# Row statistics in three groups of 8, 8 and 16 tiles in place of two of 8 and 24

## The chip, the core and the metric

The kernel runs on one core of a Trainium2 chip. The metric is the device time of one execution in microseconds (us); lower is better. The engines are called PE (TensorE, matmuls), DVE (VectorE), ACT (ScalarE), POOL (GpSimd) and SP (SyncE, which here issues all DMAs). Each engine has a queue of its own and works through it in order; engines wait for each other by semaphores.

## The reference

x is 8 batches x 512 rows x 128 columns in float32. All of it passes one block:

```python
xn = _layernorm(x)                        # (x - mean) / sqrt(var + 1e-5)
s = attention(xn)                         # relu(xn @ Wq + bq), K and V alike; 16 heads of 8,
                                          # causal, masked where a row of xn sums to 0; + xn; normalised
g = _silu(ffn(xn))                        # second layernorm of xn, @ attn_w.T + attn_b + xn, then by
                                          # 256 rows one of 8 experts: gelu(. @ w1 + b1) @ w2 + b2,
                                          # then gelu(. @ next_w.T + next_b)
return x + s * g
```

The mask asks whether a row of xn sums to exactly 0, so the kernel computes xn with a square root and a quotient refined from split high and low parts, and that costs many instructions.

## The kernel before

**Tiles and parts.** The 4096 rows are 32 tiles of 128 rows; a batch is 4 tiles (`TB`). The program has two parts with a barrier between them. The first prepares everything by batch: xn, the q and k rows (each split into three bf16 parts and stored in DRAM), v, and the gate g for all rows. The second runs the attention of the 8 batches and writes the output. The change is in the first part alone.

**DVE in the first part.** All helpers record their instructions through `link`, which makes DVE wait for the end of each instruction before it starts the next one (L313 to L317; in `quotients` only the last of four instructions that belong together is linked). They are:

- `variances(group)`, L321 to L335: row sums, mean, centred rows and variance of all tiles of a group. `row_sum` (L78 to L87) is 5 of its 13 instructions. Four of the 13 run over all columns of the group (L81, L328, L329, L330), the others over a few numbers for each tile.
- `roots(group)`, L337 to L357: square root and reciprocal, in the Newton helper (L67 to L75, 14 instructions with three steps) and 15 more. All work on one column for each tile.
- `second_roots(group)`, L377 to L384: what the second layernorm needs, 4 instructions and the Newton helper's 14.
- `quotients(i)`, L359 to L375, gives xn of batch i and releases PE's transposes. `sums(i)`, L386 to L395, gives its row sums and releases ACT's second layernorm (`sums_ready`). `rests` (L397 to L402) and `lows` (L404 to L409) are DVE's share of splitting q and k: `rests` waits for ACT's `full` and `parts[0]` (L498, L499), `lows` waits for ACT's middle part (L517) and releases SP's stores (`low_ready`). `gate(i)` (L411 to L417) finishes the gate.

`GROUPS` (L31) says which tiles are handled together: 8 tiles (batches 0 and 1), then 24 (batches 2 to 7). The order on DVE is written out by hand (L419 to L447): group 0 with `variances`, `roots`; batch 0 with `quotients`, `second_roots(GROUPS[0])`, `sums`; batch 1; the rests of batch 0; `variances(GROUPS[1])`; the low parts of batch 0; `roots(GROUPS[1])`; then a loop over the batches i = 2 to 7. A turn is `quotients(i)`, the rests of batch i-1, `sums(i)`, `gate(i-2)`, and the low parts of batch i-1; the turn of batch 2 has `second_roots(GROUPS[1])` ahead of its sums.

**The other engines.** SP loads x by group (L232 to L240), after the first group the rows of biases, after the second the weights, and behind the loop `w1` and `w2` (L241, L242). Then, by batch, it waits for `low_ready` and stores the parts of q (3 DMAs) and k (5 DMAs), and from the third batch on it also loads query and key rows for the attention part. ACT copies q and k of a batch out of PSUM (L498, L499) only when the stores of the batch before have landed (`parts_out`), then v (L503), then the experts' gelus (L511) with the middle parts between them (L517, after `rest_ready`), then the second layernorm of the next batch (L459). PE's second half of the experts (L598, h = 1) waits for v to be out of its bank (`vb_free`). Then come the transposes of the next batch (L548, L542), the products L553 and L555, q (L579) and k (L580).

Of the kernel before, what the change touches and what calls it, by code (L numbers as in the profile page):

```python
# [26 lines left out]
NT = B * T // P  # L27
TB = T // P
STEPS = B // MB
MT = NT // MB  # L30
GROUPS = ((0, 2 * TB), (2 * TB, NT - 2 * TB))  # L31
EC = T // 2
HC = HID // P
G = 4
# [32 lines left out]
def rsqrt_newton(link, dve, y, t, a, steps):  # L67

    link(dve.tensor_scalar(t.bitcast(I32), a.bitcast(I32), 1, None, ALU.logical_shift_right))  # L69
    link(dve.tensor_scalar(y.bitcast(I32), t.bitcast(I32), -1, RSQRT_SEED, ALU.mult, ALU.add))  # L70
    for _ in range(steps):
        link(dve.tensor_tensor(t, y, y, ALU.mult))
        link(dve.tensor_tensor(t, t, a, ALU.mult))
        link(dve.tensor_scalar(t, t, -0.5, 1.5, ALU.mult, ALU.add))
        link(dve.tensor_tensor(y, y, t, ALU.mult))  # L75


def row_sum(link, dve, total, s16, s8, s4, s2, src):  # L78

    add = dve.tensor_tensor  # L80
    link(dve.tensor_reduce(s16, src.rearrange("p n (k l) -> p n l k", l=16), AX.X, ALU.add))  # L81
    v = s16.rearrange("p n (a b l) -> p n a b l", a=2, b=2)
    link(add(s8, v[:, :, :, 0, :], v[:, :, :, 1, :], ALU.add))
    link(add(s4, s8[:, :, 0, :], s8[:, :, 1, :], ALU.add))
    v = s4.rearrange("p n (a b) -> p n a b", b=2)
    link(add(s2, v[:, :, :, 0], v[:, :, :, 1], ALU.add))
    link(add(total, s2[:, :, 0], s2[:, :, 1], ALU.add))  # L87
# [7 lines left out]
def build_program(nc, ctx, x, wq, wk, wv, wattn, wnext, w1, w2, cols, rows, out):  # L95
# [3 lines left out]
    def sem(name):  # L99
        return ctx.enter_context(nc.semaphore(name))  # L100
# [64 lines left out]
    with ExitStack() as one:  # L165
# [37 lines left out]

        x_in = [sem(f"x_in{k}") for k in range(len(GROUPS))]
        rows_in, bias_ready = sem("rows_in"), sem("bias_ready")
# [23 lines left out]
        with nc.Block() as block:  # L229
            @block.sync  # L230
            def _(sp):
                for k, (t0, n) in enumerate(GROUPS):  # L232
                    sp.dma_start(x_all[:, t0:t0 + n, :], x_tiles[:, t0:t0 + n, :]).then_inc(x_in[k], 16)
# [76 lines left out]
            def _(dve):  # L310
                chain = [0]

                def link(ins):  # L313

                    chain[0] += 1
                    ins.then_inc(dve_self, 1)
                    dve.wait_ge(dve_self, chain[0])  # L317
# [3 lines left out]
                def variances(group):  # L321

                    t0, n = group
                    at = slice(t0, t0 + n)
                    xg = x_all[:, at, :]
                    row_sum(link, dve, mean[:, at], s16[:, at, :], s8[:, at, :, :], s4[:, at, :], s2[:, at, :], xg)
                    link(dve.tensor_scalar(mean[:, at], mean[:, at], 1.0 / C, None, ALU.mult))
                    link(tt(cen[:, at, :], xg, mean[:, at].unsqueeze(2).broadcast_to([P, n, C]), ALU.subtract))  # L328
                    link(tt(work[:, at, :], cen[:, at, :], cen[:, at, :], ALU.mult))  # L329
                    link(dve.tensor_reduce(win[:, at, :], work[:, at, :].rearrange("p n (w k) -> p n w k", k=32),  # L330
                                           AX.X, ALU.add))
                    link(tt(var[:, at], win[:, at, 0], win[:, at, 1], ALU.add))
                    link(tt(var[:, at], var[:, at], win[:, at, 2], ALU.add))
                    link(tt(var[:, at], var[:, at], win[:, at, 3], ALU.add))
                    link(dve.tensor_scalar(a[:, at], var[:, at], 1.0 / C, 1e-5, ALU.mult, ALU.add))  # L335

                def roots(group):  # L337

                    at = slice(group[0], group[0] + group[1])
                    a_, y_, t_, s_, sh_, sl_, r_, nr_, rem_ = (v[:, at] for v in (a, y, t, s, sh, sl, r, nr, rem))  # L340

                    rsqrt_newton(link, dve, y_, t_, a_, 3)
                    link(tt(s_, a_, y_, ALU.mult))
                    link(dve.tensor_scalar(sh_.bitcast(I32), s_.bitcast(I32), TOP12, None, ALU.bitwise_and))
                    link(tt(sl_, s_, sh_, ALU.subtract))
                    link(tt(t_, sh_, sh_, ALU.mult))
                    link(tt(rem_, a_, t_, ALU.subtract))
                    link(tt(t_, sh_, sl_, ALU.mult))
                    link(dve.scalar_tensor_tensor(out=rem_, in0=t_, scalar=-2.0, in1=rem_, op0=ALU.mult, op1=ALU.add))
                    link(tt(t_, sl_, sl_, ALU.mult))  # L350
                    link(tt(rem_, rem_, t_, ALU.subtract))
                    link(tt(t_, rem_, y_, ALU.mult))
                    link(dve.scalar_tensor_tensor(out=s_, in0=t_, scalar=0.5, in1=s_, op0=ALU.mult, op1=ALU.add))
                    link(dve.tensor_scalar(sh_.bitcast(I32), s_.bitcast(I32), TOP12, None, ALU.bitwise_and))
                    link(tt(sl_, s_, sh_, ALU.subtract))
                    link(dve.reciprocal(r_, s_))
                    link(dve.tensor_scalar(nr_, r_, -1.0, None, ALU.mult))  # L357

                def quotients(i):  # L359

                    tiles = slice(TB * i, TB * i + TB)
                    cu, wu = cen[:, tiles, :], work[:, tiles, :]
                    link(tt(quo[:, :, :], cu, r[:, tiles].unsqueeze(2).broadcast_to([P, TB, C]), ALU.mult))
                    link(dve.tensor_scalar(qhi[:, :, :].bitcast(I32), quo[:, :, :].bitcast(I32), TOP12, None, ALU.bitwise_and))
                    link(tt(qlo[:, :, :], quo[:, :, :], qhi[:, :, :], ALU.subtract))
                    for in0, by, in1, op, dst in (
                            (qhi, sh, cu, ALU.subtract, wu), (qlo, sh, wu, ALU.add, wu),
                            (qhi, sl, wu, ALU.add, wu), (qlo, sl, wu, ALU.add, wu),
                            (wu, nr, quo, ALU.add, xn_all[:, tiles, :])):
                        for k in range(TB):  # L370
                            at = TB * i + k
                            ins = dve.scalar_tensor_tensor(out=dst[:, k, :], in0=in0[:, k, :], scalar=by[:, at:at + 1],
                                                           in1=in1[:, k, :], op0=ALU.mult, op1=op)
                        link(ins)
                    dve.sem_inc(xn_ready, 1)  # L375

                def second_roots(group):  # L377

                    at = slice(group[0], group[0] + group[1])
                    link(dve.tensor_scalar(v2[:, at], var[:, at], 1.0 / C, None, ALU.mult))  # L380
                    link(tt(v2[:, at], v2[:, at], r[:, at], ALU.mult))
                    link(tt(v2[:, at], v2[:, at], r[:, at], ALU.mult))
                    link(dve.tensor_scalar(v2[:, at], v2[:, at], 1e-5, None, ALU.add))
                    rsqrt_newton(link, dve, y2[:, at], t[:, at], v2[:, at], 3)  # L384
# [12 lines left out]
                def rests(tok):  # L397

                    for o in range(2):
                        dve.wait_ge(split_ready, tok.next(split_ready))  # L400
                        link(tt(rest[:, o, :], full[:, o, :], parts[:, o, 0, :], ALU.subtract))
                        dve.sem_inc(rest_ready, 1)  # L402
# [17 lines left out]
                dve.wait_ge(x_in[0], 16)  # L420
                variances(GROUPS[0])
                roots(GROUPS[0])
                quotients(0)
                second_roots(GROUPS[0])
                sums(0)
# [3 lines left out]
                rests(tok)  # L429
                variances(GROUPS[1])  # L430
                lows(tok)
                roots(GROUPS[1])
                for i in range(2, B):
                    quotients(i)
                    rests(tok)
                    if i == 2:
                        second_roots(GROUPS[1])
                    sums(i)
                    if i == B - 1:
                        link(dve.tensor_scalar(live_all[:, :], zero_all[:, :], -1.0, 1.0, ALU.mult, ALU.add))  # L440
                        dve.tensor_scalar(mask_b[:, :], zero_all[:, :], -BIG, None, ALU.mult).then_inc(mask_ready, 1)
                    gate(tok, i - 2)
                    lows(tok)
# [640 lines left out]
```

## Time and profile before

| | before |
|---|---|
| median of 3 runs | 526.83 us (526.40 to 527.27) |
| the profiled execution | 526.47 us, its span 524.7 us |
| PE busy | 437.2 us (83%), 3697 instructions |
| DVE busy | 399.6 us (76%), 976 instructions |
| ACT busy | 302.1 us (58%), 644 instructions |
| POOL busy | 126.5 us (24%), 346 instructions |
| first part (to the barrier) | 0 to 187 us of the span |
| mean granted TensorE clock | 0.942 |

Times in rows are microseconds from the start of the span, unless ns is written. A row of a timeline gives the start, the duration, the engine, the line of the kernel, the operation, the output and input with their shapes, and how many instructions were merged into the row; in brackets stands the idle time before it and what ended that. Gaps between linked instructions of under about 0.15 us are not shown as idle time. "PEclk" is the granted share of TensorE's full clock: 1.00 is 2.4 GHz, 0.50 is 1.2 GHz.

### The profile page before, as it was taken

To read this page: it belongs to the slowest core of one execution; us is meant where nothing else is said; L and a number is where in the kernel's file an instruction comes from. 1 tells how busy PE (TensorE), PEld (TensorE's weight loads), DVE (VectorE), ACT (ScalarE), POOL (GpSimd) and SP (SyncE) were. 2 spreads that over 40 slices of the span, in tenths; PEclk is the share of its full clock that TensorE was granted. 3 is DMA by queue.
4 is the path that set the end of the run, shared out by engine and by line. 5 is a ranking of instruction groups with operands and counts; after the bars stand their busy time and mean duration, and the time that the engine had idled before them with its cause. 6 is when DMAs were issued, how large, how long until landed. Compare 5 with 4: busy or idle time off the path is not lost.

```text
span 524.7 us, 10282 instructions
## 1 busy us (share of the span) xinstructions
PE 437.2 (83%) x3697; PEld 269.2 (51%) x3697; DVE 399.6 (76%) x976; ACT 302.1 (58%) x644; POOL 126.5 (24%) x346
## 2 busy tenths in 40 slices
PE   0049545999999559999999999999999999999980
PEld 0026334767667425555555556556556555555540
DVE  6989998899984267667977877877877877787606
ACT  0029134888787504556666567567567566666670
POOL 8000000000000021011155154164163163162281
PEclk9999957999999955899999999999999999999996
DMA  8900021244443200122312312213323213222000
GB/s 231 296 0 0 11 71 31 60 122 125 126 126 82 81 6 24 51 69 49 93 48 69 92 49 79 82 48 90 74 47 101 61 48 111 52 48 67 3 22 20
DMA packets 27433, 37.60 MB, mean 72 GB/s; under 512 B 5622, under 2 KB 19830, under 8 KB 27382
## 3 DMA queue, kind: packets, MB, share of 16 engines
q1 hardware_dynamic: 27382, 36.94, 25.9%
q8 instruction: 29, 0.48, 0.4%
q14 instruction: 22, 0.18, 0.1%
HBM read 25.91 MB, written 10.49 MB: 69 GB/s over the span
## 4 chain that ended last, share of the span: by engine, by line
PE 53%; DVE 9%; issue 1%; ACT 1%; DVEq 0%; ACTq 0%
PE banks L963 15%; PE banks L994 14%; PE banks L982 12%; PE banks L965 5%; PE banks L984 5%; DVE mx L816 5%; PE banks L1004 1%; DVE stats L863 1%; DVE aggr L867 1%; ACT pt L934 0%; DVE bits L69 0%; DVE seed L70 0%; PE banks L972 0%; DVE half L894 0%; DVE res L850 0%
## 5 line engine op out<-in xcount | busy, mean ns | idle before, releaser
L816 DVE TENSOR_REDUCE mx<-banks 128x1 f32<-128x384 f32 (+3 forms) x384 | 211.1, 597 | 63.6 <-PE banks L965 58.4
L934 ACT ACTIVATE pt<-banks 128x512 f32<-128x512 f32 (+2 forms) x384 | 184.8, 528 | 110.8 <-PE banks L984 99.9
L965 PE MATMUL banks<-causal,ident_b 128*128 128x128 bf16 x512 | 106.8, 228 | 0.0
L984 PE MATMUL banks<-causalT,ident_b 128*128 128x128 bf16 x512 | 103.8, 222 | 0.0
L963 PE MATMUL banks<-k_own,q_own 73*128 73x512 bf16 (+3 forms) x256 | 75.3, 331 | 11.2 <-DVEq L896 8.6
L994 PE MATMUL banks<-pt,vg 128*18 128x512 f32 (+3 forms) x1024 | 82.4, 440 | 0.5 <-ACT pt L934 0.5
L963 PE MATMUL banks<-w_room 73*128 73x512 bf16 (+3 forms) x256 | 69.0, 302 | 3.4 <-DVE mx L816 3.4
L982 PE MATMUL banks<-q_own,k_own 76*128 76x512 bf16 (+3 forms) x256 | 71.1, 310 | 0.0
L982 PE MATMUL banks<-w_room 76*128 76x512 bf16 (+3 forms) x256 | 67.7, 300 | 1.2 <-ACT pt L934 1.2
L726 POOL TENSOR_SCALAR mneg<-mx 128x16 f32<-128x16 f32 x32 | 8.1, 253 | 192.7 <-DVEq L824 192.7
L965 PEld LDWEIGHTS banks<-causal,ident_b 128*128 128x128 bf16 x512 | 52.1, 102 | 0.0
L984 PEld LDWEIGHTS banks<-causalT,ident_b 128*128 128x128 bf16 x512 | 50.9, 99 | 0.2
L963 PEld LDWEIGHTS banks<-k_own,q_own 73*128 73x128 bf16 x256 | 26.2, 104 | 44.3 <-issue 18.7
L598 PE MATMUL banks<-xaT,w_room 128*128 128x256 f32 x128 | 32.3, 400 | 16.9 <-ACT v_all L503 16.9
L994 PEld LDWEIGHTS banks<-pt,vg 128*18 128x18 f32 x1024 | 23.8, 97 | 39.3 <-issue 29.1
L789 POOL MEMSET vg<- 128x1152 f32 x1 | 1.1, 1057 | 173.5 <-POOLq L229 173.5
L963 PEld LDWEIGHTS banks<-w_room 73*128 73x128 bf16 x256 | 24.6, 97 | 33.0 <-DVE mx L816 13.6
L598 PEld LDWEIGHTS banks<-xaT,w_room 128*128 128x128 f32 x128 | 24.3, 199 | 22.3 <-ACT v_all L503 19.3
L610 PE MATMUL banks<-hid,w_room 128*128 128x256 f32 x128 | 32.2, 406 | 3.3 <-ACT hid L511 3.3
L982 PEld LDWEIGHTS banks<-w_room 76*128 76x128 bf16 x256 | 25.0, 98 | 15.6 <-ACT pt L934 4.7
L982 PEld LDWEIGHTS banks<-q_own,k_own 76*128 76x128 bf16 x256 | 25.8, 101 | 12.9 <-ACT pt L934 2.2
L610 PEld LDWEIGHTS banks<-hid,w_room 128*128 128x128 f32 x128 | 25.7, 205 | 8.7 <-ACT hid L511 4.5
(155 smaller groups left out, 581.1 us busy)
## 6 DMA issues: line engine op xcount, KB each, us to landing
k_scratch<-parts SPq DMA_DIRECT2D x40, 128.0 KB, 2.4
q_own<-q_scratch SPq DMA_DIRECT2D x48, 96.0 KB
k_own<-k_scratch SPq DMA_DIRECT2D x48, 96.0 KB
w_room<-q_scratch SPq DMA_DIRECT2D x48, 96.0 KB
w_room<-k_scratch SPq DMA_DIRECT2D x48, 96.0 KB
q_scratch<-parts SPq DMA_DIRECT2D x24, 128.0 KB, 2.4
w_room<-in_w_dram SPq DMA_DIRECT2D x1, 2048.0 KB, 9.2
out_dram<-mixed SPq DMA_DIRECT2D x7, 256.0 KB, 2.5
```

The lines of the kernel that those rows point to most:

```text
L598: ins = mm(banks[:, bank + j // 2, EC * (j % 2):EC * (j % 2) + EC], w1_sb[:, 2 * n + h, P * j:P * j + P], xaT[:, EC * h:EC * h + EC], star ...
L610: ins = mm(banks[:, XB, EC * h:EC * h + EC], w2_sb[:, 2 * n + h, j, :], hid[:, h, j, :], start=(j == 0), stop=(j == HC - 1))
L726: link(pool.tensor_scalar(mneg[:, 0], mx[:, u % 2].rearrange("p h n -> p (h n)"), -1.0, None, ALU.mult))
L816: ins = dve.tensor_reduce(mx[:, u % 2, heads[0]:heads[-1] + 1, q], banks[:, S0 + c % RING, 0:w * len(heads)].rearrange("p (h k) -> p h k", ...
L863: ins = dve.bn_stats(stats[:, k, :], res[:, k, :])
L867: ins = dve.bn_aggr(aggr[:, k, :], stats[:, k, :])
L934: act.activation(weights(k, heads[0], len(heads)), banks[:, ST0 + j % RING, 0:(T - P * k) * len(heads)], ACT.Exp, scale=SCALE).then_inc(ex ...
L963: mm(o, qx[by][0:MROW + 1, g, h, P * q:P * q + P], kx[by][0:MROW + 1, g, h, 0:w], start=True, stop=False)
L965: ins = mm(o[:, w - P:w], ident_b[:, :], causal[:, :], start=False, stop=True)
L982: mm(o, kx[par][0:STACK, g, h, P * k:P * k + P], qx[par][0:STACK, g, h, P * k:T], start=True, stop=False)
L984: ins = mm(o[:, 0:P], ident_b[:, :], causalT[:, :], start=False, stop=True)
L994: ins = mm(banks[32 * h:32 * h + VP, OT, P * k:T], vg[:, g, k, h, :], pt[:, PT0[k] + h * n:PT0[k] + h * n + n], start=(k == 0 and g % 2 == 0),
```

## The change

`GROUPS` gets three entries, so SP loads x with three DMAs (the weights follow the second of them, as before), and there is a third semaphore for the third load. On DVE the second group is now 8 tiles (batches 2 and 3). The remaining 16 tiles (batches 4 to 7) get their load wait, `variances` and `roots` at the top of batch 4's turn, ahead of its quotients, and their `second_roots` in that turn, ahead of its sums. Nothing else is changed, in neither part.

```diff
-GROUPS = ((0, 2 * TB), (2 * TB, NT - 2 * TB))
+GROUPS = ((0, 2 * TB), (2 * TB, 2 * TB), (4 * TB, NT - 4 * TB))
...
                 lows(tok)
                 roots(GROUPS[1])
                 for i in range(2, B):
+                    if i == 4:
+                        dve.wait_ge(x_in[2], 16)
+                        variances(GROUPS[2])
+                        roots(GROUPS[2])
                     quotients(i)
                     rests(tok)
-                    if i == 2:
-                        second_roots(GROUPS[1])
+                    if i % 2 == 0 and i <= 4:
+                        second_roots(GROUPS[i // 2])
                     sums(i)
```

## Rows read from the trace of the kernel before

**Rows 1.** DVE's waits, 4.6 to 163.4: waited for, us in total, times, longest

```profile
DVE s L81 <- DMA x_all<-in_x_dram: 4.6, 1, 4.6
```

**Rows 2.** DVE's waits, 4.6 to 187: the longest of the others

```profile
DVE rest L401 <- ACT parts L499: 7.8, 2, 5.6
```

**Rows 3.** Busy us (instructions) of each engine in one batch's period; clock, DMA share, GB/s

```profile
104.20:118.90 14.70, 14.14 (x69) 10.27 (x68) 13.20 (x36) 12.43 (x27) 0.00 (x0) 1.00 0.43 113
```

**Rows 4.** DVE's timeline: the blocks of 24 tiles, rests and low parts, two batch starts

```profile
45.04 5.37 DVE L81 TENSOR_REDUCE s<-x_all 128x384 f32<-128x3072 f32 x1
...
62.89 1.53 DVE L408 TENSOR_TENSOR parts<-rest,parts 128x512 bf16<-128x512 f32 x2
64.56 0.18 DVE L69 TENSOR_SCALAR small<-small 128x24 int32<-128x24 int32 x1
...
70.95 0.69 DVE L363 TENSOR_TENSOR quo<-xn_all,small 128x512 f32<-128x512 f32 x1
...
78.85 1.53 DVE L401 TENSOR_TENSOR rest<-full,parts 128x512 f32<-128x512 f32 x2
80.53 0.18 DVE L380 TENSOR_SCALAR small<-small 128x24 f32<-128x24 f32 x1
...
84.42 1.00 DVE L81 TENSOR_REDUCE s<-xn_all 128x64 f32<-128x512 f32 x1
...
97.42 1.53 DVE L401 TENSOR_TENSOR rest<-full,parts 128x512 f32<-128x512 f32 x2
...
104.23 0.69 DVE L363 TENSOR_TENSOR quo<-xn_all,small 128x512 f32<-128x512 f32 x1
...
118.94 0.69 DVE L363 TENSOR_TENSOR quo<-xn_all,small 128x512 f32<-128x512 f32 x1
```

**Rows 5.** DVE's timeline: the blocks of the first group, 8 tiles

```profile
4.59 1.86 DVE L81 TENSOR_REDUCE s<-x_all 128x128 f32<-128x1024 f32 x1 [4.59 <-DMA x_all<-in_x_dram]
...
11.44 0.48 DVE L332 TENSOR_TENSOR small<-win 128x8 f32<-128x8 f32 x1
...
12.65 0.25 DVE L69 TENSOR_SCALAR small<-small 128x8 int32<-128x8 int32 x1
...
18.71 0.69 DVE L363 TENSOR_TENSOR quo<-xn_all,small 128x512 f32<-128x512 f32 x1
...
26.61 0.17 DVE L380 TENSOR_SCALAR small<-small 128x8 f32<-128x8 f32 x1
...
30.27 1.00 DVE L81 TENSOR_REDUCE s<-xn_all 128x64 f32<-128x512 f32 x1
```

**Rows 6.** ACT's timeline: split copies of batches 1 and 2

```profile
67.41 0.69 ACT L498 ACTIVATE full<-banks,cols_sb 128x512 f32<-128x512 f32 x1 [11.11 <-DMA q_scratch<-parts]
...
71.28 0.68 ACT L499 ACTIVATE parts<-banks,cols_sb 128x512 bf16<-128x512 f32 x1
...
96.81 0.70 ACT L499 ACTIVATE parts<-banks,cols_sb 128x512 bf16<-128x512 f32 x1
```

**Rows 7.** Busy us in short stretches; the third number from the end is PE's clock

```profile
66.00:69.00 3.00, 0.00 (x0) 0.00 (x0) 2.51 (x15) 1.27 (x2) 0.00 (x0) 0.50 0.73 203
...
90.00:92.00 2.00, 2.00 (x11) 1.85 (x11) 1.90 (x6) 0.97 (x2) 0.00 (x0) 0.56 0.72 197
```

**Rows 8.** PE's timeline: L553 in batches 0 and 2, the hole, attention's first product

```profile
36.28 2.08 PE L553 MATMUL banks<-xlT,wattn_sb 128*128 128x512 f32 x2 [0.87 <-ACT xlT L470]
...
72.50 3.78 PE L598 MATMUL banks<-xaT,w_room 128*128 128x256 f32 x8 [12.88 <-ACT v_all L503]
...
92.07 1.02 PE L553 MATMUL banks<-xlT,wattn_sb 128*128 128x512 f32 x2
...
188.93 0.58 PE L963 MATMUL banks<-k_own,q_own 73*128 73x512 bf16 x1 [8.65 <-DVEq L896]
```

**Rows 9.** DVE's unlinked L372: four merged, then the durations of one (ns, min/median/max)

```profile
72.86 1.14 DVE L372 SCALAR_TENSOR_TENSOR gate_all<-qhi,small,xn_all 128x128 f32<-128x128 f32 x4
...
L372 DVE SCALAR_TENSOR_TENSOR gate_all<-qhi,small,xn_all x32: 346/347/352, 20.6 to 151.1; 128x128 f32<-128x128 f32 x32
```

## The prediction

> **What bounds the kernel now.** The span is 524.7 us, and the edit touches only the part of it ahead of 187 us (preparation and gate); the attention loop behind it is started by a barrier and keeps its work. So I ask which engine sets the length of the first part. I read the list of waits of VectorE (DVE) first [rows 1]: from its first instruction at 4.59 us to 163.4 us it has not one wait but the load of x that it starts with. The reader is to see that this list is empty otherwise: a queue of linked instructions that never waits for another engine is the bound itself. The same list to 187 us [rows 2] adds waits, all of them behind the last batch's rows, the longest 7.8 us for ScalarE's (ACT's) split copies. Then I read the busy times by batch [rows 3], because they could speak against this: in 104.2 to 118.9 us TensorE (PE) is busy 14.14 of 14.70 us, DVE only 13.20. The 1.5 us missing on DVE are the gaps of about 0.03 to 0.15 us between an instruction and the next one that is linked to it; they are part of its pace. The batch period is DVE's own, L363 to L363, 118.94 - 104.23 = 14.71 us [rows 4]. By the code PE waits for ACT in each batch (`vb_free`), ACT for the stores of the batch before (`parts_out`), and SP with those stores for DVE's low parts (`low_ready`). The circle closes at DVE. The end of the first part hangs on DVE as well: the last batch's splits wait for the stores that DVE's second-last low parts release. What is added to DVE's queue before 163.4 us therefore moves the end of the first part one for one, unless DVE is left waiting somewhere, which adds more.
>
> **The change, part by part.**
>
> *Loads.* The third load of x costs SP one more issue, with the weights now behind the second load in place of the third. The first load and its wait are as before. DVE asks for the third group some 50 us later than it asked for all 24 tiles in the kernel before, where the wait showed nothing [rows 1]. I cost it at nothing: the cover is DVE's own work of the first two batches, and if it were gone the price would be one issue, under 1 us.
>
> *One group of 24 becomes 8 and 16.* This repeats `variances` (13 linked DVE instructions: 5 of the row sum, 8 more), `roots` (14 of the Newton helper with three steps, 15 more: 29) and `second_roots` (4 and 14: 18): 60 instructions more. The elements are the same, so what is added is the part of each instruction that doesn't grow with its width. Rows give it by block. `second_roots` takes 84.42 - 80.53 = 3.89 us for 24 tiles [rows 4] and 30.27 - 26.61 = 3.66 us for 8 [rows 5]. On a straight line its part without width is 3.66 - (3.89 - 3.66)/2 = 3.55 us, or 0.197 us for each of 18 instructions. `roots` takes 70.95 - 64.56 = 6.39 and 18.71 - 12.65 = 6.06 us, so 5.90 without width (0.203 each). `variances` takes 62.89 - 45.04 = 17.85 and 12.65 - 4.59 = 8.06 us, so 3.17 without width (0.244 each). The last two are from the kernel's first microseconds, where single instructions were stretched: L332 on 8 columns took 0.48 us [rows 5], more than twice the 0.197. I take the undisturbed rate for all: 60 x 0.197 = 11.8 us. The high end is the sum of the three blocks as they stand, 3.17 + 5.90 + 3.55 = 12.6. The low end gives the four wide instructions of `variances` what L81 shows without width: (5.37 - 1.86)/2 = 1.755 for 1024 columns, 0.11 of 1.86 left, with a gap of 0.03 some 0.14; that is 56 x 0.197 + 4 x 0.14 = 11.6 us.
>
> *What moves.* The 8-tile blocks take about 7.6 and 5.9 us in place of 17.85 and 6.39. The first low parts, which release batch 0's stores, then start near 52.7 in place of 62.89 us, and batch 2's rows begin near 60.2 in place of 70.95. ACT's wait for those stores, now 11.11 us ahead of L498 at 67.41 [rows 6], shrinks, and with it the PE hole behind it. None of that is worth anything: DVE did not wait in that stretch, so what is late next is DVE itself, as before. In exchange the 16-tile blocks (by the line between 8 and 24: 12.7, 6.2 and 3.8 us, 22.7 together) stand in DVE's queue behind batch 2's low parts. Queued behind the first two of them (18.9 us) are batch 4's quotients, batch 3's rests, then its gate and low parts, and behind these SP's stores of batch 3 and its loads of query and key rows. ACT waits for the rests of batch 3, PE for ACT. All of these are off DVE's queue, and DVE gets back to them with its inputs long there.
>
> *Where DVE could be left waiting.* Batch 1's rests (L401) come at 78.85 us and the last split they need ends at 71.28 + 0.68 = 71.96 [rows 6], 9.1 us behind the start of the low parts at 62.89 [rows 4]. After the change the splits end near 52.7 + 9.1 = 61.8, the rests stand at 52.7 + 1.7 + 5.9 + 7.9 = 68.2: margin 6.4, no wait. The margin one batch later is thin. The second of batch 2's two rests starts half of 1.53 and a gap behind 97.42, near 98.26 [rows 4], and the split they need ends at 96.81 + 0.70 = 97.51: 0.75 us [rows 6]. This chain runs from DVE's sums over ACT and PE back to DVE, the DVE work beside it is the same after the change, and batch 4 (behind the new hole) goes through it in the same order. If it keeps its length, the cost is 0. If PE is slower in it, DVE waits.
>
> *The clock in that chain.* PE's granted clock is 0.50 in 66 to 69 us, inside the 12.88 us in which PE had nothing to do ahead of L598 at 72.50, and 0.56 in 90 to 92 us [rows 7, 8]; the products from 92.07 on run at the full rate, 1.02 us for L553 [rows 8]. So in the kernel before this chain runs in part at 1.2 GHz and ends at 2.4. The worst case is what batch 0 had: there the same L553 took 2.08 us [rows 8], 1.06 more. Three such products stand in the chain (L553, L555, L579). Work ahead of them brings the clock back, so I let two of them be slow: 2.1 us, less the margin of 0.75, is 1.4 us for a batch. The change leaves PE with nothing for about 18 us ahead of batch 4, and less than now ahead of batch 2. The Trainium skill ("TensorE: Matmul & The Clock Gate", Part 1, What's actually happening) says that the slow clock is the default and that activity releases it, which speaks against a change that leaves such a hole; by it alone the sum would take this case.
>
> *Sum.* The profiled execution took 526.47 us: 524.7 of span and 1.77 around it. 526.47 + 11.8 + 0 = 538.3. The median of the runs shown is 0.36 higher, 526.83, which gives 538.6 us. I forecast 538.6.
>
> **The rivals.**
>
> *A. The low clock leaves DVE waiting.* As above, at batch 4, at batch 2 or at both: 0 to 1.4 us each, on top of 11.8. For it: the hole, and a margin of 0.75 us only. Against it: the kernel before has a hole of 12.88 us in front of L598 at 72.50 [rows 8] and still kept the margin. Time: 538.6 to 541.4, about 539.6.
>
> *B. PE sets the pace, the other side.* If from 89 us on PE and not DVE were the bound, batch 2's rows 10.9 us earlier would be a gain of 10.9, and the 22.7 us of the 16-tile blocks would be covered by one batch of work in hand, 14.7 us, and cost 8.0: 526.8 - 2.9 = 523.9 us, faster. It decides from the point where the other engines hold more than 22.7 - 10.9 = 11.8 us of work when DVE turns to the third group. For it speaks PE busy 14.14 of 14.70 us [rows 3]. Against it: a DVE queue without a wait [rows 1] can't be ahead of anything; its own instructions fill the time, and 60 more of them can't be put anywhere before the end.
>
> *C. The added instructions overlap.* Four unlinked L372 instructions of 0.347 us each take 1.14 us together [rows 9], so they start (1.14 - 0.347)/3 = 0.26 us apart and hide 0.08 each; if the 60 hid as much and had no gap, they would cost 60 x (0.197 - 0.03 - 0.08) = 5.2 us: 532.0 us. Against it: each of the 60 waits for the end of the one before it by its link, and 18 of them in a row take 3.66 us [rows 5], 0.203 each, with nothing hidden. The Trainium skill ("Vector Engine (DVE) Microarchitecture Reference", section 5.2) states about 75 ns per instruction after queue overlap, by which the sum would be 60 x 0.075 = 4.5 us, some 531.3 us; the trace differs, with 0.197 for linked ones.
>
> **How the numbers follow.** Forecast (11.6 to 12.6 us, no wait on DVE): 0.67. A: 0.28. B: 0.015. C: 0.02. The rest, 0.015, is left for a mishap that I can't name. Forecast with the spread of the runs (526.40 to 527.27): 538.0 to 539.9. To hold 8 in 10, the range must take in more than half of A: up to 540.8, and at the low end a little for wide instructions cheaper than the rows: 537.6. A measurement of this kernel can tell about 0.2% (1.1 us) from no change; B is below that, so faster 0.02; hardly any case lies within it, 0.01; slower 0.97, since the forecast, A and C are all above 527.9.
>
> **What the profile after would show.** The DVE list of waits empty between its first load and a last low part near 175.2 us: right; a row DVE L401 <- ACT L499 at batch 2 or 4 with 0.1 to 1.5 us: case A, with a granted clock near 0.5 beside it. `variances` of 16 tiles near 12.7 us, `roots` 6.2, `second_roots` 3.8, small instructions still 0.20 us apart; 0.1 would be C. Batch 2's quotients near 60 us, those of batch 4 ending near 120, a hole of about 18 us on PE before them. The barrier and the first attention product 11.8 us later than 188.93 [rows 8], and the attention part as long as before. If the first part is not longer by the added DVE time, the reading that DVE is its bound is wrong, and with it the prediction.

## The result and the profile after

The changed kernel takes 537.42 us (median of five runs, 537.30 to 538.34) against 526.83 us (five runs, 526.25 to 527.63). The ratio on record is 1.0213, 95% interval 1.0201 to 1.0225; the plain quotient of the two medians, 1.0201, lies at its lower end. It is slower by about 11 us. The profiled execution took 537.33 us with a span of 535.6 us, 10.9 us over the span before.

The page of the profile after, the lines that answer to the table of before (busy time, share of the span, instructions):

```profile
span 535.6 us, 10343 instructions
...
PE 439.4 (82%) x3697; PEld 271.3 (51%) x3697; DVE 409.1 (76%) x1036; ACT 301.9 (56%) x644; POOL 125.9 (24%) x346
```

The instruction counts say it at once: DVE has 1036 instructions where it had 976, which are the 60 repeated ones; PE, ACT and POOL have theirs unchanged.

DVE's waits, 4.6 to 174 us (answers to [rows 1]), and behind it the longest of the list to 199 us (answers to [rows 2]):

```profile
DVE s L81 <- DMA x_all<-in_x_dram: 4.5, 1, 4.5
...
DVE rest L401 <- ACT parts L503: 7.4, 2, 5.2
```

DVE's timeline at the borders of the blocks (answers to [rows 4]):

```profile
44.92 1.89 DVE L81 TENSOR_REDUCE s<-x_all 128x128 f32<-128x1024 f32 x1
...
52.55 1.53 DVE L408 TENSOR_TENSOR parts<-rest,parts 128x512 bf16<-128x512 f32 x2
54.23 0.17 DVE L69 TENSOR_SCALAR small<-small 128x8 int32<-128x8 int32 x1
...
60.13 0.69 DVE L363 TENSOR_TENSOR quo<-xn_all,small 128x512 f32<-128x512 f32 x1
...
86.38 1.53 DVE L401 TENSOR_TENSOR rest<-full,parts 128x512 f32<-128x512 f32 x2
...
93.19 3.65 DVE L81 TENSOR_REDUCE s<-x_all 128x256 f32<-128x2048 f32 x1
...
105.96 0.17 DVE L69 TENSOR_SCALAR small<-small 128x16 int32<-128x16 int32 x1
...
112.10 0.69 DVE L363 TENSOR_TENSOR quo<-xn_all,small 128x512 f32<-128x512 f32 x1
...
121.69 0.17 DVE L380 TENSOR_SCALAR small<-small 128x16 f32<-128x16 f32 x1
...
125.46 1.01 DVE L81 TENSOR_REDUCE s<-xn_all 128x64 f32<-128x512 f32 x1
...
173.33 1.53 DVE L408 TENSOR_TENSOR parts<-rest,parts 128x512 bf16<-128x512 f32 x2
```

The reader is to see three things. First, the empty list: DVE still waits for nobody before the last batch. Second, the blocks: `variances` took 52.55 - 44.92 = 7.63 us for 8 tiles and 105.96 - 93.19 = 12.77 for 16; `roots` 5.90 and 6.14. `second_roots` took 3.66 (69.71 to 73.37 in the same timeline) and 125.46 - 121.69 = 3.77. Together that is 39.87 us where [rows 4] had 28.13: 11.74 us more. Third, batch 6's low parts begin at 173.33 us; in the kernel before they began at 161.69. That is 11.64 later (the stretch began 0.12 earlier).

PE's timeline (answers to [rows 8]) shows what the move did on the other side of the circle:

```profile
63.38 2.49 PE L602 MATMUL banks<-xaT,w_room 128*128 128x256 f32 x8 [3.70 <-ACT v_all L507]
...
122.93 3.58 PE L614 MATMUL banks<-hid,w_room 128*128 128x256 f32 x8 [17.02 <-ACT hid L515]
```

The hole of 12.88 us ahead of batch 1's second half has shrunk to 3.70 us, and a new one of 17.02 us stands inside batch 3, ahead of the second half of the experts' second product (L614): PE waits there for ACT's gelus, and ACT for DVE's rests. The earlier start of batch 2, 10.8 us on DVE (60.13 against 70.95), was real and brought nothing.

### The profile page after: what moved, and what is told of

The parts are those of the page before. It is cut to its first block, busy times and chain, and to the rows that moved or that the text cites. A ratio compares the mean times of both kernels' runs of the same rounds, so it can differ in the third digit from the quotient of the medians.

```text
span 535.6 us, 10343 instructions
## 1 busy us (share of the span) xinstructions
PE 439.4 (82%) x3697; PEld 271.3 (51%) x3697; DVE 409.1 (76%) x1036; ACT 301.9 (56%) x644; POOL 125.9 (24%) x346
## 4 chain that ended last, share of the span: by engine, by line
PE 52%; DVE 9%; issue 1%; ACT 1%; DVEq 0%; ACTq 0%
PE banks L967 14%; PE banks L998 13%; PE banks L986 12%; PE banks L969 5%; PE banks L988 5%; DVE mx L820 5%; PE banks L1008 1%; DVE stats L867 1%; DVE aggr L871 1%; ACT pt L938 0%; PE banks L976 0%; DVE seed L70 0%; DVE bits L69 0%; DVE half L898 0%; DVE res L854 0%
## 5 line engine op out<-in xcount | busy, mean ns | idle before, releaser
L614 PE MATMUL banks<-hid,w_room 128*128 128x256 f32 x128 | 34.0, 421 | 19.6 <-ACT hid L515 19.6
L614 PEld LDWEIGHTS banks<-hid,w_room 128*128 128x128 f32 x128 | 26.6, 212 | 25.6 <-ACT hid L515 21.2
L602 PE MATMUL banks<-xaT,w_room 128*128 128x256 f32 x128 | 30.8, 388 | 6.5 <-ACT v_all L507 6.5
```

The lines of the kernel that those rows point to most:

```text
L602: ins = mm(banks[:, bank + j // 2, EC * (j % 2):EC * (j % 2) + EC], w1_sb[:, 2 * n + h, P * j:P * j + P], xaT[:, EC * h:EC * h + EC], star ...
L614: ins = mm(banks[:, XB, EC * h:EC * h + EC], w2_sb[:, 2 * n + h, j, :], hid[:, h, j, :], start=(j == 0), stop=(j == HC - 1))
```

## The experiments

Ratios are to the kernel before, on the same chip. "The barrier" is the start of the attention part's first DVE instruction (`half`): 186.82 us in the kernel before, 198.06 in the changed one. The kernel before was timed anew beside the experiments, with medians of 526.04 to 526.42 us; "over before" and "under before" are meant against these.

The kernel before, batch 6's low parts and the barrier on DVE's timeline:

```profile
161.69 1.53 DVE L408 TENSOR_TENSOR parts<-rest,parts 128x512 bf16<-128x512 f32 x2
...
186.82 1.24 DVE L894 TENSOR_SCALAR half<-rows_sb 128x256 f32<-128x256 f32 x1 [4.44 <-PEq L229]
```

The barrier in the changed kernel:

```profile
198.06 1.24 DVE L898 TENSOR_SCALAR half<-rows_sb 128x256 f32<-128x256 f32 x1 [4.43 <-PEq L229]
```

### The added instructions or their place?

```diff
-GROUPS = ((0, 2 * TB), (2 * TB, NT - 2 * TB))
+GROUPS = ((0, 2 * TB), (2 * TB, 2 * TB), (4 * TB, NT - 4 * TB))
...
                 variances(GROUPS[1])
+                variances(GROUPS[2])
                 lows(tok)
                 roots(GROUPS[1])
+                roots(GROUPS[2])
...
                         second_roots(GROUPS[1])
+                        second_roots(GROUPS[2])
```

> The kernel before with the three groups of the change, but all blocks of the third group stand directly behind those of the second, where the 24-tile blocks stood (about 45 to 84 us); nothing is moved behind batch 3. Same 60 instructions more than before, no hole ahead of batch 4. Theory (DVE's queue is the bound, the added linked instructions cost 0.197 us each wherever they stand): 11 to 12 us over before, within 0.7 us of the changed kernel. Rival (the place costs: the hole of 17 us on PE and ACT behind batch 3 is what was paid): little over before, at most 4 us.

Measured: 538.19 us, ratio 1.0226 (1.0199 to 1.0254); the barrier at 198.29 us. The same as the changed kernel, with nothing placed behind batch 3. So the price is that of the 60 instructions; the hole that they left on PE and ACT, wherever it stood, cost nothing that these two times can tell apart. One line of DVE's timeline is new:

```profile
109.89 0.69 DVE L401 TENSOR_TENSOR rest<-full,parts 128x512 f32<-128x512 f32 x1 [0.21 <-ACT parts L503]
```

This is case A of the prediction in small: here DVE waited 0.21 us for batch 2's split. PE's timeline shows L557 (L553 before) at 1.53 us in that chain, partly at the low clock, where it took 1.02 in [rows 8].

### The same instructions where DVE waits, and where it doesn't

```diff
+                def extra(n, linked):
+                    for k in range(n):
+                        ins = tt(spare[:, k, :], a[:, 0:8], a[:, 0:8], ALU.mult)
+                        if linked:
+                            link(ins)
```

Called as `extra(24, True)` behind the loop, ahead of the last `rests`:

> The kernel before with 24 linked multiplications of 8 columns added on DVE, on a spare tile, behind the low parts of batch 6 and ahead of the last rests, where DVE waits 5.64 us for ACT. Theory: 24 x 0.203 = 4.9 us lie inside that wait, 0 to 0.3 us over before. Rival (each DVE instruction costs its time wherever it stands, as issue or by disturbing the other engines): 4.9 us over before.

Called as `extra(24, True)` at the top of the turn i = 4:

> The same 24 multiplications at the top of batch 4's turn, ahead of its quotients, where the changed kernel has its third group. Theory: 4.6 to 4.9 us over before, all of it. Rival (PE sets the pace in the batches and DVE has work in hand for them): 0 to 2 us over before.

The 24 instructions in the wait, and then in the queue, on DVE's timelines of the two kernels:

```profile
163.23 4.79 DVE L423 TENSOR_TENSOR spare<-small 128x8 f32<-128x8 f32 x24
168.63 0.69 DVE L402 TENSOR_TENSOR rest<-full,parts 128x512 f32<-128x512 f32 x1 [0.61 <-ACT parts L508]
```

```profile
104.18 4.79 DVE L423 TENSOR_TENSOR spare<-small 128x8 f32<-128x8 f32 x24
109.00 0.69 DVE L364 TENSOR_TENSOR quo<-xn_all,small 128x512 f32<-128x512 f32 x1
```

In both they took 4.8 us of DVE's time. Behind the loop they turned a wait of 5.64 us into one of 0.61: 526.77 us, ratio 1.0012 (1.0000 to 1.0024), the barrier at 186.57, no later than before. In the queue: 531.35 us, ratio 1.0097 (1.0077 to 1.0118), the barrier at 191.58, 4.76 us later. That is 24 x 0.20 us, paid in full. The same instructions cost at most 1.3 us (the upper end of the interval) on one side of 163.4 us, with nothing of it at the barrier, and their whole time on the other, as the empty list of [rows 1] says.

### What the link is worth

Called as `extra(60, False)` at the top of the turn i = 4:

> Sixty multiplications of 8 columns at the top of batch 4's turn, each on columns of its own and none linked, so DVE doesn't wait for the end of one before the next. It measures what the link is worth. If an unlinked small instruction hides about 0.08 us and leaves no gap, as L372 does, they are some 0.09 us apart: 5 to 6 us over before. If the fixed time of an instruction is its own and not the link's, 0.17 to 0.20 us apart: 10 to 12 us over before.

```profile
104.01 4.71 DVE L423 TENSOR_TENSOR spare<-small 128x8 f32<-128x8 f32 x60
108.64 0.68 DVE L364 TENSOR_TENSOR quo<-xn_all,small 128x512 f32<-128x512 f32 x1
```

Sixty in 4.63 us, 0.077 us apart, against 0.20 with the link: 530.43 us, ratio 1.0084 (1.0059 to 1.0109). That is 4.2 us over before, under the 5 to 6 us that the expectation gave for a spacing of 0.09 us. Case C had the size of an unlinked instruction too high, with 0.087 us. The Trainium skill ("Vector Engine (DVE) Microarchitecture Reference", section 5.2) has about 75 ns per instruction after queue overlap, beside a part that grows with the columns; for unlinked ones this run agrees. Of the 0.20 us that a small linked instruction costs, 0.12 us goes with waiting for the end of its predecessor. The 60 instructions of the change depend on each other, so whether they could be spared that wait was not tried.

### The change turned around

One group of 32 tiles; x still arrives in four loads of 8 tiles (`LOADS`), and `row_sum` starts its first reduction in pieces behind them. The loads of the biases and weights follow the last of the four.

```diff
+        for (t0, n), loaded in pieces:
+            dve.wait_ge(loaded, 16)
+            link(dve.tensor_reduce(s16[:, t0:t0 + n, :],
+                                   src[:, t0:t0 + n, :].rearrange("p n (k l) -> p n l k", l=16), AX.X, ALU.add))
...
-                variances(GROUPS[0])
-                roots(GROUPS[0])
+                variances(ALL)
+                roots(ALL)
                 quotients(0)
-                second_roots(GROUPS[0])
+                second_roots(ALL)
                 sums(0)
                 quotients(1)
                 sums(1)
-                dve.wait_ge(x_in[1], 16)
                 rests(tok)
-                variances(GROUPS[1])
                 lows(tok)
-                roots(GROUPS[1])
...
-                    if i == 2:
-                        second_roots(GROUPS[1])
```

> The opposite of the change: one group of 32 tiles. variances, roots and second_roots run once, so 60 linked instructions fewer than in the kernel before; x is loaded in four pieces of 8 tiles and the first row-sum reduction runs in four pieces behind them (3 instructions more); batch 0's low parts follow its rests directly, where variances of 24 tiles stood between them. Theory: 60 x 0.197 = 11.8 us less on DVE, 0.4 us for the pieces, and some 3 to 4 us of new waits where the 24-tile block had covered ACT's middle parts of batch 0: 7 to 9 us under before, 517.5 to 520 us. Rival (first rows late: PE and ACT start their first batch some 18 us later and set the end): at or over before.

Measured: 519.66 us, ratio 0.9875 (0.9854 to 0.9896), the barrier at 179.74: 7.1 us earlier. It beats both kernels. DVE's waits, 4 to 190 us, and the two rows of its timeline where the new ones stand:

```profile
DVE rest L409 <- ACT parts L501: 7.4, 2, 5.5
DVE parts L416 <- ACT parts L519: 6.5, 4, 3.0
...
65.08 0.69 DVE L416 TENSOR_TENSOR parts<-rest,parts 128x512 bf16<-128x512 f32 x1 [2.96 <-ACT parts L519]
67.05 0.69 DVE L416 TENSOR_TENSOR parts<-rest,parts 128x512 bf16<-128x512 f32 x1 [1.28 <-ACT parts L519]
```

Of the 11.8 us that 60 instructions fewer are worth, 4.2 us went to DVE's wait for batch 0's middle parts, which the 24-tile block had covered. PE's first transposes came at 43.56 us in place of 26.67, and the kernel is faster all the same.

The next run filled those 4.2 us with DVE work that stood behind them: `quotients(2, 0)` is the first three instructions and the first two of the five rounds of four, `quotients(2, 1)` the other three rounds.

```diff
                 rests(tok)
+                quotients(2, 0)
                 lows(tok)
+                quotients(2, 1)
+                sums(2)
                 for i in range(2, B):
-                    quotients(i)
+                    if i > 2:
+                        quotients(i)
                     rests(tok)
-                    sums(i)
+                    if i > 2:
+                        sums(i)
```

> The kernel with one group of 32 tiles (519.66 us), with the 4.2 us that DVE waits for batch 0's middle parts filled: the first half of batch 2's quotients stands ahead of these low parts, and batch 2's sums stand ahead of batch 1's rests. Theory: there it is ACT's chain (rests of batch 0 to the splits of batch 1, 15.5 us) that is late next, so the wait moves to batch 1's rests and only 0 to 1.5 us are won: 518.2 to 519.7 us. Rival (DVE alone is the bound there too): 4 us won, 515.7 us.

Measured: 519.81 us, ratio 0.9870 (0.9850 to 0.9891), the barrier at 179.25. That is 0.5 us earlier at the barrier and nothing in the time. The wait moved, as DVE's timeline shows at batch 1's rests and low parts:

```profile
76.82 0.69 DVE L412 TENSOR_TENSOR rest<-full,parts 128x512 f32<-128x512 f32 x1 [1.79 <-ACT parts L509]
...
79.28 0.69 DVE L419 TENSOR_TENSOR parts<-rest,parts 128x512 bf16<-128x512 f32 x1 [0.92 <-ACT parts L527]
81.25 0.69 DVE L419 TENSOR_TENSOR parts<-rest,parts 128x512 bf16<-128x512 f32 x1 [1.28 <-ACT parts L527]
```

In that one stretch others are the bound, not DVE. The last two rows are waits for ACT's middle parts, which stand between the gelus in its queue. The first wait has a store behind it, as the row of ACT's copy of batch 1's k shows:

```profile
75.52 0.69 ACT L508 ACTIVATE full<-banks,cols_sb 128x512 f32<-128x512 f32 x1 [1.55 <-DMA k_scratch<-parts]
```

In the kernel with one group this copy began at 74.80 us and waited for nothing. Here `quotients(2, 0)` lasted longer than the wait that it filled: batch 0's first low part began at 66.40 us in place of 65.08, and SP's stores behind it at 67.18 in place of 65.86. So part of the wait that came in place of the old one was made by the filling itself, for which the expectation had no term. Whether a shorter piece of work ahead of the low parts would win something was not tried.

### How much room the others have

Every batch's k product done twice:

```diff
                     mm(banks[:, QB, :], wq_sb[:, :], xT, start=True, stop=True).then_inc(q_done, 1)
+                    mm(banks[:, KB, :], wk_sb[:, :], xT, start=True, stop=True)
                     mm(banks[:, KB, :], wk_sb[:, :], xT, start=True, stop=True).then_inc(k_done, 1)
```

> The kernel before with the product of the k rows (two passes, 0.86 us) done twice in each of the 8 batches on PE, the first result overwritten. It measures how much slack PE and ACT have behind DVE. Theory (DVE's queue is the bound, with a margin of 0.75 us at batch 2 and more where the stores are waited for): only batch 2 is late by 0.1 us or so, and the last batch not at all; 0 to 0.5 us over before. Rival (PE, busy for 14.1 of 14.7 us, is the bound or shares it): 0.86 us for each of batches 2 to 7, 5.2 us over before.

Measured: 527.19 us, ratio 1.0019 (1.0009 to 1.0029), about 1.0 us over before, where the rival asked for 5.2 us. The profiled execution (525.81 us, the fastest of its kernel) shows no wait of DVE before the last batch and the barrier at 186.03, so it does not show where the timed 1 us lies. That stays open. PE did 6.9 us more in this part (8 x 0.86) for about a seventh of it; by the interval the price was 0.5 to 1.5 us.

The gate's instruction left out of DVE, its waits and releases kept:

```diff
                     dve.wait_ge(tah_ready, tok.next(tah_ready))
-                    link(dve.scalar_tensor_tensor(out=gate_all[:, TB * i:TB * i + TB, :].rearrange("p n c -> p (n c)"),
-                                                  in0=tah[:, :], scalar=1.0, in1=gel[:, :],
-                                                  op0=ALU.add, op1=ALU.mult))
                     dve.sem_inc(gate_done, 1)
```

> The kernel before without the gate's instruction (0.69 us, 0.84 with its gap) on DVE or anywhere; the waits and the releases stay. Left out: the gate of all rows, so the output lacks it. DVE's queue is 0.84 us shorter in each of batches 2 to 7, and nothing runs on POOL. It tells whether moving the gate to POOL failed by a clash of POOL with DVE or because PE and ACT were the bound. Theory (DVE's queue sets the pace): 3 to 5 us under before. Rival (PE and ACT are at the bound too): 0 to 1 us under before.

Measured: 523.63 us, ratio 0.9942 (0.9923 to 0.9961), the barrier at 183.84, 2.98 us earlier. DVE's queue lost 5.0 us; 1.3 us came back as waits for splits at batches 2 and 3, as these rows of its timeline show, and about 1 us as gaps of 0.17 to 0.4 us in DVE's own queue ahead of the low parts:

```profile
96.82 0.69 DVE L401 TENSOR_TENSOR rest<-full,parts 128x512 f32<-128x512 f32 x1 [0.27 <-ACT parts L496]
97.97 0.69 DVE L401 TENSOR_TENSOR rest<-full,parts 128x512 f32<-128x512 f32 x1 [0.46 <-ACT parts L496]
...
112.39 0.69 DVE L401 TENSOR_TENSOR rest<-full,parts 128x512 f32<-128x512 f32 x1 [0.54 <-ACT parts L496]
```

Work taken from DVE is worth about 60% here, work given to it 100%. PE and ACT are close behind at batches 2 and 3, at batch 2 in part by the low clock (the product that took 1.02 us at 92.07 in [rows 8] took 1.22 here). Behind them DVE waited for no split before the last batch, and its period fell from 14.71 to 14.02 us (117.85 to 131.87). And the gate moved to POOL in place of left out, on the kernel before and on the one with one group (`gate` is gone from DVE):

```diff
+                for i in range(B):
+                    pool.wait_ge(tah_ready, tok.next(tah_ready))
+                    out_i = gate_all[:, TB * i:TB * i + TB, :].rearrange("p n c -> p (n c)")
+                    link(pool.tensor_tensor(out_i, tah[:, :], gel[:, :], ALU.mult))
+                    link(pool.tensor_tensor(out_i, out_i, gel[:, :], ALU.add))
+                    pool.sem_inc(gate_done, 1)
```

> The kernel before with the gate moved from DVE (one instruction of 0.69 us, 0.84 with its gap) to POOL, which is idle there, as a product and a sum. DVE's queue is 0.84 us shorter in each of batches 2 to 7, 5.0 us before its last wait. Theory (DVE's queue sets the pace and the others have some slack): up to 5.0 us under before; if the other engines' slack in a steady batch is smaller than 0.84 us, DVE begins to wait in its rests and the gain is 3 to 5 us. Rival (PE and ACT at the bound too, so that nothing taken from DVE is worth anything): 0 to 1 us under before.

> The kernel with one group of 32 tiles, and the gate on POOL as well. Theory: both savings add, 3 to 5 us under the kernel with one group (519.7), so 514.5 to 516.7 us, as long as PE and ACT follow. Rival (with one group the other engines are already the bound in the batches): 518.5 to 520 us.

Measured: 531.71 us, ratio 1.0101 (1.0084 to 1.0118), and 526.87 us, ratio 1.0006 (0.9996 to 1.0015). Both expectations missed by far and with the wrong sign: the move costs 5 us on the kernel before, and 7 us on the one with one group. DVE and POOL in the first of the two kernels:

```profile
55.17 3.36 DVE L336 TENSOR_TENSOR gate_all<-xn_all 128x3072 f32<-128x3072 f32 x1
56.83 2.83 POOL L310 TENSOR_TENSOR gate_all<-tah,gel 128x512 f32<-128x512 f32 x1 [43.52 <-ACT tah L482]
...
109.61 1.35 POOL L310 TENSOR_TENSOR gate_all<-tah,gel 128x512 f32<-128x512 f32 x1 [11.01 <-ACT tah L482]
109.86 3.12 DVE L379 SCALAR_TENSOR_TENSOR gate_all<-qlo,small,gate_all 128x128 f32<-128x128 f32 x4
111.04 1.27 POOL L311 TENSOR_TENSOR gate_all<-gate_all,gel 128x512 f32<-128x512 f32 x1
```

Four instructions that take 1.14 us together [rows 9] took 3.12 us while POOL ran its two. The durations of single ones in 111 to 112.4 us (ns, min/median/max) say how:

```profile
L379 DVE SCALAR_TENSOR_TENSOR gate_all<-qlo,small,gate_all x3: 339/1247/1421, 109.9 to 112.4; 128x128 f32<-128x128 f32 x3
```

One is undisturbed, two took 1.25 and 1.42 us. The first rows show the other direction: a POOL instruction that took 1.27 us in most batches took 2.83 beside a DVE instruction of 3.36 us. Leaving the gate out gave 3 us, moving it lost 5, and the clash accounts for the difference: in the turns of batches 3 to 7 DVE's instructions beside POOL's took 9.9 us longer than without them, 5.0 us were spared, and batch 6's low parts began at 166.75 us in place of 161.69. POOL's gate ran as soon as ACT's `tah` was there, beside DVE's quotients; whether it would clash less in another place was not tried.

## Why the prediction was right, point by point

The forecast was 538.6 us, or 538.3 for the profiled execution; measured were 537.42 and 537.33. The range that was to hold 8 in 10, 537.6 to 540.8, holds 526.83 times the ratio on record, 538.05 us; the bare median lies 0.2 us below it. The mechanism and its main term came as forecast, and what made the sum some 1 us too high is the last point of this list.

- *DVE's queue is the bound.* Shown from both sides: 24 instructions in the queue cost 4.76 us at the barrier and in the wait behind it nothing (the pair above); PE's added 6.9 us cost about 1. One reading was off without harm: in [rows 2] 7.8 us is the sum of two waits, and the longest is 5.6.
- *60 instructions at 0.197 us, 11.8 us.* Measured 11.74 by the blocks. The reason for taking `second_roots` and not the higher sum of 12.6 held: in the new place `variances` of 8 tiles took 7.63 us where the first group's took 8.06. The stretched L332 of [rows 5] stands again at 0.47 us in the same place of the changed kernel, and it starts inside a POOL instruction; after the POOL experiment that is the likely cause, though no run isolated it.
- *The third load, at nothing.* Right: DVE's list has no wait for it. The weights stand behind the second load in both kernels, not "in place of the third"; the new load is issued behind them.
- *Earlier starts are worth nothing, what is late next is DVE.* Right: 10.8 us earlier at batch 2, the hole shrunk to 3.70 us, no gain. With all blocks in the old place and no earlier start the time was the same.
- *The margin at batch 2 and the clock (case A).* The second of batch 2's rests started half of 1.53 and a gap behind 86.38 us, near 87.22; its split ended at 86.28 + 0.70 = 86.98 (ACT's timeline). The margin fell from 0.75 to 0.24 us. PE's granted clock was 0.53 in 79 to 82 us, in that chain, although the long hole ahead of it had shrunk, and L557 took 1.28 us. So the thought that a shorter hole is safe was wrong; with the blocks in place the margin went 0.21 us below zero. At batch 4 it was 138.47 + 0.84 - (137.92 + 0.70) = 0.69 us, behind 17.02 us of nothing on PE. So A had a mechanism that exists and its place the wrong way round. Rows show why the long hole was not what counted: the granted clock was 0.50 in 110 to 120 us, 1.00 again in 127 to 129 behind the products of L614, and 0.50 in 130 to 133, behind the next hole of 2.99 us. The Trainium skill's rule from the prediction ("TensorE: Matmul & The Clock Gate", Part 1) agrees with this, low without work and full behind it, but it does not lead to case A, as the prediction thought. A hole of some 3 us stands ahead of the chain in each case (3.13 us in the kernel before, 3.23 and 2.99 in the changed one), and its first transposes took 1.07 to 1.11 us each time. What differs is when the clock came back: L572 (L576 after) took 1.60, 1.91 and 1.71 us. What sets that stays open here. DVE's waits behind products at the low clock were none in these two kernels, 0.21 us with the blocks in place and 0.73 at batch 2 without the gate.
- *Case B* is excluded by the added 24 instructions and by the doubled product, *case C* by the linked instructions 0.20 us apart.
- *The 0.9 us missing* (11.8 forecast, 10.9 more span). 11.64 us at batch 6's low parts became 11.24 at the barrier: the last batch's wait for its stores was 5.2 us in place of 5.6 [rows 2]. From the barrier to the end of the span it took 535.6 - 198.06 = 337.54 us against 524.7 - 186.82 = 337.88, 0.34 less. In the other kernels, which leave this part alone, it took 337.7 to 338.6 us, so I read it as spread. The prediction had no term for either.

## What to carry to other kernels

An engine whose list of waits is empty over a whole stage is its bound, even at 90% busy: here each instruction added to its queue cost its whole time, and starts made earlier for the others were worth nothing. Work taken from it was worth less (3.0 of 5.0 us), since waits appear that the list did not have. Splitting a block of narrow, dependent instructions repeats their fixed part, here 60 x 0.2 us, so the question for such blocks is how to merge them: one group of 32 tiles, with only the first reduction cut into pieces behind the loads, ran in 519.66 us, 6 us under the kernel before and 18 under the changed one. What a merge uncovers must be read from the waits afterwards, since part of the gain (4.2 of 11.8 us) goes to the transfer or chain that the block had hidden.

## What the runs showed of the hardware

- DVE and POOL hold each other up: during a POOL instruction of 1.35 us on two SBUF tensors, a DVE instruction of 0.35 us with two tensor inputs took 1.25 us, and a POOL instruction of 1.27 us took 2.83 beside a DVE instruction of 3.36. The Trainium skill ("SBUF — State Buffer", Terms) says that the two engines share a port pair with an exclusive lock held for the full instruction; the rows agree. Here an idle POOL was not free help for a DVE at its bound.
- Small DVE instructions of 8 columns start 0.077 us apart when nothing links them and 0.20 us apart when each waits for the one before it.
- The granted TensorE clock in a chain did not follow the length of the longest hole ahead of it. In the changed kernel batch 2's chain stood behind holes of 3.70, 2.17 and 3.23 us with short work between them, batch 4's behind 17.02 and 2.99; in both the first transposes ran at the low clock (1.11 and 1.07 us, 0.66 at the full one), and L557 took 1.28 us in the first and 1.02 in the second.
